# The second layer's one-hots from two tensors: a 32-bit column row against broadcast places

## The reference

```python
edge_index = jnp.stack([src, dst])
h = jnp.maximum(_layernorm(x, axis=-1), 0.0)
x = x + _L0_gnn_ref(h, ...)                     # attention over the edges of each end
h = jnp.maximum(_layernorm(x, axis=-1), 0.0)
agg = jax.ops.segment_sum(h[src], dst, num_segments=n_nodes)
deg = jax.ops.segment_sum(jnp.ones_like(dst), dst, num_segments=n_nodes)
x = x + jnp.where((deg > 0)[:, None], agg, h)
```

## Time and profile before

| | |
|---|---|
| median of 3 runs | 1539.13 us (1538.59 to 1542.61) |
| the profiled execution's own time | 1539.34 us |
| its span, first to last instruction | 1535.5 us |
| busy over the span: PE, DVE, ACT, POOL | 1323.8, 1357.6, 1322.6, 1063.9 us |
| mean granted TensorE clock | 0.969 |
| first gather of the second layer starts | 993.49 us |
| last gather of the second layer starts | 1509.90 us |

### The profile page before, as it was taken

One profiled execution on the slowest core, in us unless ns is written; L12 is line 12 of the kernel. 1 busy time (PEld: TensorE's weight loads), 2 busy tenths in 40 slices (PEclk: granted clock), 3 DMA queues, 4 the chain that ended last, 5 costly groups with the idle time before them and its releaser, 6 DMA issues.

```text
span 1535.5 us, 34345 instructions
## 1 busy us (share of the span) xinstructions
PE 1323.8 (86%) x12142; PEld 1286.2 (84%) x12143; DVE 1357.6 (88%) x3631; ACT 1322.6 (86%) x3488; POOL 1063.9 (69%) x959
## 2 busy tenths in 40 slices
PE   1599999999999999999999999557777778777786
PEld 0589999999999999999999999457777778777676
DVE  6669999999999999999999988938888888888786
ACT  0688999899999999999999998269899999999897
POOL 5678888877667677886776730177777777777772
PEclk9999999999999999999999999869898999999999
DMA  4876877788787777887788766628899999998875
GB/s 118 239 185 157 205 207 213 212 220 181 208 219 214 209 192 214 221 208 205 202 220 206 199 179 177 183 75 249 238 253 252 256 250 251 259 254 249 241 219 150
DMA packets 465930, 321.99 MB, mean 210 GB/s; under 512 B 31008, under 2 KB 433010, under 8 KB 465758
## 3 DMA queue, kind: packets, MB, share of 16 engines
q1 hardware_dynamic: 434526, 257.32, 62.2%
q0 software_dynamic: 31232, 62.49, 14.7%
HBM read 215.19 MB, written 104.45 MB: 208 GB/s over the span
## 4 chain that ended last, share of the span: by engine, by line
PE 47%; POOL 27%; DVE 10%; issue 10%; ACT 2%; DMA 2%; POOLq 0%; SPq 0%; DVEq 0%; ACTq 0%
POOL xe L1171 18%; PE c_p L1700 7%; PE c_p L1701 6%; POOL xn L1171 5%; PE c_p L1703 5%; PE t_p L1688 4%; POOL xe L1163 3%; PE t_p L1686 3%; PE t_p L1682 3%; PE y_p L1716 3%; PE y_p L1718 3%; PE y_p L1719 3%; PE y_p L1717 3%; PE t_p L1685 3%; DVE st L1285 2%
## 5 line engine op out<-in xcount | busy, mean ns | idle before, releaser
L1163 POOL DMA_INDIRECT xe<-in_x,idx_t x516 | 643.0, 1246 | 213.6 <-issue 138.8
L1171 POOL DMA_INDIRECT xe<-x_d,idx x308 | 300.6, 976 | 126.3 <-issue 92.7
L1603 ACT ACTIVATE an<-xn,nbias,rstd 128x128 f32<-128x128 f32 x783 | 326.6, 482 | 3.9 <-DVE nbias L1316 3.9
L1606 ACT ACTIVATE ae<-xe,nbias,rstd 128x128 f32<-128x128 f32 x522 | 226.2, 482 | 0.0
L1285 DVE BATCH_NORM_STATS2 st<-xe 128x6 f32<-128x256 f32 x422 | 166.9, 413 | 55.6 <-DMA xe<-x_d,idx 55.2
L1700 PE MATMUL c_p<-w1a,th 128*128 128x129 f32 x1044 | 215.7, 288 | 0.0
L1701 PE MATMUL c_p<-w1b,th 128*128 128x129 f32 x1044 | 202.5, 276 | 0.0
L1285 DVE BATCH_NORM_STATS2 st<-xn 128x6 f32<-128x256 f32 x440 | 169.7, 413 | 34.5 <-DMA xe<-in_x,idx_t 16.8
L1402 DVE TENSOR_SCALAR sel<-row,plc_t,alpha 128x256 f32<-128x256 bf16 x522 | 190.6, 405 | 3.4
L1703 PE MATMUL c_p<-relk,ot 128*128 128x129 bf16 x1566 | 176.8, 221 | 0.0
L1701 PEld LDWEIGHTS c_p<-w1b,th 128*128 128x128 f32 x1044 | 159.1, 193 | 0.0
(11 more groups left out here) (221 smaller groups left out, 3614.6 us busy)
## 6 DMA issues: line engine op xcount, KB each, us to landing
xn<-in_x SPq DMA_DIRECT2D x130, 384.0 KB, 7.1
x_d<-xn SPq DMA_DIRECT2D x130, 384.0 KB, 8.9
xn<-x_d SPq DMA_DIRECT2D x194, 256.0 KB, 4.5
out<-xn SPq DMA_DIRECT2D x194, 256.0 KB, 3.6
plr<-place_d SPq DMA_DIRECT2D x65, 464.0 KB
tyr<-types_d SPq DMA_DIRECT2D x65, 256.0 KB
xe<-in_x,idx_t POOLq DMA_INDIRECT x522
xe<-x_d,idx POOLq DMA_INDIRECT x308
```

Of the source, the lines that this page charges most:

```text
L1163: nc.gpsimd.indirect_dma_start(out=xe_of(u)[:, e, :], out_offset=None, in_=x, in_offset=bass.IndirectOffsetOnAxis(ap=idx_t[:, j:j + 1], ax ...
L1171: nc.gpsimd.indirect_dma_start(out=xe2_of(u)[:, e, :], out_offset=None, in_=x1_d, in_offset=bass.IndirectOffsetOnAxis(ap=idx2[:, j:j + 1], ...
L1603: a(an[:, u % 2, i, :], xs_of(u)[:, i, :], ACT.Relu, bias=nbias1[:, c:c + 1], scale=rstd1[:, c:c + 1])
L1606: last = a(ae[:, u % 2, e, :], xe_of(u)[:, e, :], ACT.Relu, bias=nbias1[:, c:c + 1], scale=rstd1[:, c:c + 1])
```

## The change

The operation of L1413 gets another form, and the column row another type. Before, it is a `tensor_scalar`: one tensor (the column row as bf16), and two scalars of each partition read from SBUF (the place, and a one), with a comparison and a multiplication. After, it is a `tensor_tensor`: two tensors, the column row as 32-bit numbers, and the place, which is repeated over the columns by a stride of zero, with the comparison alone. The result is 32-bit in both and has the same values. Number, order and sizes of the operations, and all waits, stay as they are. `row2` now takes the whole first buffer of `th`, and the one `iota` that fills it writes 32-bit numbers.

```diff
-        row2 = th[:, 0, 0:2 * P].bitcast(bf16)
+        row2 = th[:, 0, 0:4 * P]
...
-                        last = v.tensor_scalar(sel2_of(u, at, n), row2[:, c * P:c * P + n], plc2[:, j:j + 1], ones[:, 0:1], ALU.is_equal, ALU.mult)
+                        last = v.tensor_tensor(sel2_of(u, at, n), row2[:, c * P:c * P + n], plc2[:, j:j + 1].to_broadcast([P, n]), ALU.is_equal)
```

## The result

The changed kernel takes 1565.3 us (median of 4 runs, 1563.4 to 1566.9) against 1538.9 beside it: a ratio of 1.0165, with a 95% interval of 1.0152 to 1.0177. It is slower, as forecast, but by 26 us and not by 166: 11 us above the first rival's 1540 to 1554, and within its top of 1586.

The account below looks back on a forecast made before the run. POOL's 404 second-layer gathers were taken as the bound: 1539.3 - 14.7 (old holds) + 174 (train-end waits) + 5.6 (start) + 1 (tail) = 1705 us. The forecast's own range was 1648 to 1762, extended down to 1545 for the first rival.

Parts of the forecast that it names:

- the first rival: Second layer: a gather gets in between two operations of a train; 1540 to 1554 us, top 1586; chance 0.14.
- What bounds the layer: Second layer: POOL runs 404 gathers one after the other without pause, 516.5 of 517.6 us.
- the trains: Second layer, DVE: a unit's five L1413 operations back to back, 2.31 us before, 2.64 us forecast; 92 counted.
- DVE's own time: L1413: 685 ns at 512 columns, 422 at 256; some 32 us more on DVE, hidden, cost nothing.
- DVE's waits for landings: Sign in the second layer: DVE's idle time for landings, 55.6 us before in one group, should grow by over 100 us.
- DMA's share: Sign in the second layer: DMA's share should have fallen from 0.84.
- What is held, and by what: Second layer: operations on two SBUF tensors hold a gather, which ends about 0.82 us after release; L1413's old 14.7 us go.
- The second rival: Second layer: a broadcast operand takes nothing a gather needs, all 404 take 0.94 us; 1526 us; chance 0.08.
- a gather that starts in a train waits for the train's end: Second layer: each of 92 trains catches one gather, which loses 1.27 to 2.51 us, 1.89 in the middle; 174 us.
- the pairs of the earlier trace: First layer: two-tensor operations back to back (L1513 then L1313; L1362 then L1513); gathers ended 0.82 us after the last.
- The start: Start of the second layer: three trains back to back until 999.2 us make the first gather wait 5.6 us.
- The tail: Behind the last gather: three trains left, each 0.33 us longer, 1 us.

Follow-up runs that it names:

- merged kernel: Against the changed kernel, a unit's three 512-column operations made as one of 1536, leaving three operations a train: 1618.2 us, ratio 1.0514.

## Why the prediction went wrong

**What bounds the layer**: right. POOL's stretch grew by 23.0 us and its gathers by 23.3, and without the trains it fell to the 1526 us that 944 ns a gather give.

**DVE's own time**: right. 688 to 691 and 420 to 430 ns for 685 and 422; L1413 went from 212.8 to 246.1 us, 33 more for 32. It was hidden, as forecast. DVE's waits for landings did not grow by 100 us but stayed near 55: POOL's stretch grew by 23 us only, and DVE's own work in it by 31, at the cost of its other waits. The 581 ns of before were no price of the operation alone: with no gather beside it it takes 538, and gathers that get in draw it out to as much as 745. Taken alone, the new form (688) costs 150 ns more at 512 columns. The sum came out right because the 581 already held some 40 ns of waiting for gathers, and after the change an operation waits 2 ns on average. A train is 2.56 us long, for 2.64. DMA's share fell from 0.84 to 0.80.

**What is held, and by what**: right. An operation on two tensors in SBUF holds a gather that is under way, also when one tensor is a broadcast of one number per partition, and the gather ends 0.81 to 0.82 us after it is let go. The second rival (gathers free) is refuted by 84 held ones. What it is that the operation holds stays open: a gather also reads a column of `idx2` in SBUF, and no run tells that read from the writing of descriptors. On operations with two tensors the Trainium skill, "SBUF — State Buffer", section "Who interferes with whom", and the rows differed, and the chip bore out the rows: the `tensor_tensor` of this change adds 25 us to the making of the descriptors of 404 DMAs. The same section does let such an operation contend with a GpSimd instruction that reads SBUF, and the read of the index would be one.

**The step that failed is "a gather that starts in a train waits for the train's end".** It was priced at 92 x 1.89 = 174 us. In its place 77 of 84 held gathers waited for one operation, 23.8 us, and six in the middle of the layer for a train's end, 9.0 us: 33 us for 174. Another 59 started together with an operation and cost nothing, which neither the forecast nor a rival had. I had read the rule from the pairs of the earlier trace rows, and such pairs behave so throughout: in the trace of before 35 gathers of the first layer come upon one, and in the trace after the change 44, and every one waits for the end of the second operation. But they were carried to a train of five alike, against the one row that shows a train, where the gather got in. That row I had set aside because the form was another. The merged kernel decides between the two: operations three times as long, in trains no longer, add 54 us to the gathers (93.2 for 39.4).

**The start** was forecast at 5.6 us of waiting and measured at 5.4: there the train-end rule held. **The tail** was forecast at 1 us and measured at 0.8.

**The first rival** was nearest, with its sum somewhat low. The kernel before was a poorer witness for it than it seemed: 39 of its 93 held gathers got in during an operation and not between two. It has -14.7 + 15 to 29; measured, the same parts are 23.8, inside, with 14.4 us of train-end waits and 1.2 of crumbs that it did not have: +24.7.

The Trainium skill, "SBUF — State Buffer", section "Who interferes with whom", makes the loser wait for one whole instruction. For 77 gathers the traces agree, for seven they don't: 1.3 to 5.4 us, in operations of at most 0.70. Nor do they agree for the 39 of before that got in while an operation ran.

**What stays open** is why a few gathers miss every boundary. The runs show that it happens in rows of operations without a pause. It happened to the first gather of the layer in every kernel with such rows of two tensors (5.0 to 6.1 us), and with one scalar (3.1). The kind of the operations on two tensors hardly matters (six to nine such gathers in each of five kernels), but in the merged kernel, with three operations in a train, it was the first gather alone. With 59 ns of another operation between them there was none. They do not show what sets those few gathers apart, nor why in the first layer, where L1513 or L1313 follows another operation on two tensors, no gather got in between.

## What to carry to other kernels

Where GpSimd's making of descriptors sets the pace, price an edit of VectorE by what its form does to the descriptors in the making, and only then by its length: here the shortest form (495 ns) lost 10 us, and the longest (742 + 81) won 13 us of gathers, which DVE's late finish then took back. Watch for operations on two tensors in rows without a pause; a short other operation between them, or a form that holds nothing in most of them, was worth more here than a faster one, as long as VectorE kept some waiting to spend. Look also at where the DMAs fall against the operations, since a held one depends on that as much as on the form. And a rule read from two rows of another stage is a rival, not the forecast, when a row of the stage itself speaks against it.

## What the runs showed of the hardware that I had not expected

- A gather that an operation on two tensors holds waits to the end of that operation (0.31 us on average), or, a few of them, to the end of all that stand back to back (up to 6.1 us, over some 18 operations of 0.42).
- A 59 ns `memset` of one column between the operations took the gathers' excess from 39.4 to 14.3 us, with 391 of them for 23.1 us of VectorE: the waits over several operations went, and 97 gathers in place of 18 fell into the last 160 ns of an operation.
- Waiting goes both ways. A gather that starts at most 11 ns behind the start of a `tensor_tensor` is free (59 of 59), and the operation takes 726 ns for 685; from 19 ns on it is held (83 of 83 with over 160 ns of the operation left). An operation with two scalars lets a gather in while it runs, and takes 590 ns for 540.
- The accumulating `tensor_scalar` holds no gather (944 ns for each of 404), for 742 ns in place of 576 to 581, and 81 for the sum.
- A `tensor_scalar` with one scalar takes 491 to 495 ns at 512 columns where two scalars take 576 to 581, and still cost the gathers more: 25.4 us for 14.7.
